# Second layer of a graph network: components of an outer product summed on TensorE in place of GpSimd

## The chip, the cores and the metric

The kernel runs on one core of a Trainium2 chip. The metric is the device time of one execution in microseconds (us). Three runs without a profile give a median of 7314.14 us. Everything is in fp32.

## The reference

Two graph layers run one after the other over the same 200,000 edges and 12,500 nodes of 160 features. A node's features are 64 scalars (s) and 32 vectors of 3 components (v). A layer makes a message for each edge, sums the messages by node, forms a bilinear update of each node, and normalises:

```
msg  = linear and bilinear functions of x[dst] and the edge's 4 attributes
agg  = segment_sum(msg, src)             # a0: 64 scalars, a1: 32 x 3
u0   = sum_uv xs[u] a0[v] Wu_ss[u,v,:] + sum_uv (sum_i xv[u,i] a1[v,i]) Wu_vv[u,v,:]
u1_i = sum_uv xs[u] a1[v,i] Wu_sv[u,v,:] + sum_uv xv[u,i] a0[v] Wu_vs[u,v,:]
x    = layernorm(x + x + u + linear(x))
```

The change is about the inner sum over i in the second term of u0. For each node it is a table q of 32 x 32 = 1024 numbers: the outer product of xv and a1 for each of the three components i, summed over the three. The table is then multiplied with Wu_vv (1024 x 64).

## The kernel before

The nodes are cut into 100 tiles of 125. There are three stages: the messages of the first layer, chunk by chunk; a sweep over node tiles of the first layer in which the messages of the second are made as well; and a sweep over the node tiles of the second layer alone (`node_sweep`, steps t = 0 to 101). Only the last is touched. It fills the span from about 6870 us to the end.

In step t of the last sweep the edges of tile t are summed, and tile n = t - 1 is updated. Each engine has a queue of its own, worked off in the order in which the code is written; they meet at semaphores. No planner reorders anything. The parts that matter:

- GpSimd, `node_step` (from line 651): for tile n, two mixed products `mixed_mul` (line 667, two instructions each) from ScalarE's copies `prods_sb`; then, for tile t, the outer product `outer` (line 647): q3 gets three blocks of 1024 per node, one for each component; then two additions (line 676) that sum blocks 1 and 2 into block 0. They count up the semaphore `q_part`.
- TensorE, `node_step` (from line 1157): six pairs of products `bilinear(0..5)` (lines 1177 and 1178), which alternate between two PSUM tiles `prods_ps`, so each waits until VectorE or ScalarE has used the one before the last. After the fifth comes `turn_q(0)`, then the sixth, then `sum_edges` (lines 1211 and 1212: 17 products of one-hot matrices with messages), `turn_q(1)`, `linear` (lines 1220 to 1224) and `turn_y` (lines 1231 to 1233).
- `turn_q(part)` turns half of q: 4 blocks of 128 columns by 125 nodes go to `turn_ps` as 128 x 125 each. In the second layer it is 4 transposes (line 1197) of the summed block. In the first layer it is 12 products with the identity (line 1200), three accumulated for each block, so that TensorE makes the sum over the components while it turns.
- ScalarE: copies the fifth and the sixth pair for GpSimd (`prods_out`, line 1467), copies turned q to SBUF (`turned_q`, line 1475), sums and turned y likewise (lines 1482 to 1502), then makes the one-hot matrices of the next tile (lines 1575 and 1581).
- VectorE: four rounds of product and sum for the scalar part (lines 954 and 960), its share of the mixed products (line 972), the sums of the mixed products (line 983, the second of which waits for GpSimd), and h (line 1000), which ends the tile.

Of the kernel before, what the change touches and what calls it, by code (L numbers as in the profile page):

```python
# [6 lines left out]
ALU = mybir.AluOpType  # L7
# [6 lines left out]
P = 128  # L14
# [3 lines left out]
HM = 125  # L18
# [36 lines left out]
VV = V * V  # L55
# [30 lines left out]
def build(nc, x, src, dst, attr, weights, out):  # L86
# [41 lines left out]
    with ExitStack() as whole:  # L128
        def sb(name, shape, dt=F32, ctx=whole):
            return ctx.enter_context(nc.sbuf_tensor(name, shape, dt))  # L130

        def sem(name):
            return whole.enter_context(nc.semaphore(name))

        def bank(name, n=1):
            return whole.enter_context(nc.psum_tensor(name, [P, 512 * n], F32))
# [3 lines left out]
        turn_ps = bank("turn_ps")  # L140
# [21 lines left out]
        for layer in range(2):  # L162
            t = Named()
# [77 lines left out]
        q3 = sb("q3", [P, 3 * VV])  # L241
# [30 lines left out]
        def layer_sems(layer):  # L272
            s = {}
            for n in ("hot", "edges_done", "y_out", "y_turned", "y_turned_out", "prods", "prods_used", "upd", "q_mul",
                      "q_turned", "q_turned_out", "lin", "lin_out", "h_ready", "deviation", "inverse", "normed",
                      "msg", "pay_out", "located", "slotted",
                      "t_turned", "t_turn_out", "t_mm", "t_out", "first_fill",
                      "sp_ids", "sp_link", "sp_index", "sp_rec", "sp_keys", "sp_tab", "sp_sum", "sp_old", "sp_put", "sp_done"):
                s[n] = sem(f"{n}_l{layer}")
            for n in (("picked", "pick_turned", "pick_out"), ("copied", "mixed_mul", "q_part"))[layer]:  # L280
                s[n] = sem(f"{n}_l{layer}")
            for n in ("msgs_in", "x_in", "stored", "spill_in", "rec_in", "t_stored", "filled"):
                s[n] = [sem(f"{n}{b}_l{layer}") for b in range(2)]
            for n in ("win_in", "scattered"):
                s[n] = [sem(f"{n}{q}_l{layer}") for q in range(4)]
            return s

        LS = [layer_sems(layer) for layer in range(2)]
        block = whole.enter_context(nc.Block())

# [35 lines left out]
        def within(k, lo, hi):  # L326

            return not isinstance(k, int) or lo <= k < hi
# [5 lines left out]
        def earlier(k):  # L334
            c, ck, cb = k
            return (c - 1, ck - 1, 1) if cb == 0 else (c - 1, ck, 0)
# [218 lines left out]
        def _(g):  # L555
# [23 lines left out]
            def scatter(layer, k, hh):  # L579

                c, ck, cb = k
                s, q = LS[layer], 2 * cb + hh
                g.wait_ge(s["located"], 2 * c + hh + 1)
                g.wait_ge(s["slotted"], 2 * c + hh + 1)
                if within(c, 2 - 2 * layer, STRIPS[layer]):
                    g.wait_ge(s["filled"][cb], 32 * ck + 32 * layer)
                for p in range(PAIRS):
                    g.wait_ge(s["pay_out"], 8 * c + 4 * hh + p + 1)
                    carry()
                    for j in (2 * p, 2 * p + 1):  # L590
                        g.indirect_dma_start(out=slots[layer][:, :], out_offset=bass.IndirectOffsetOnAxis(ap=slot[q][:, j:j + 1], axis=0),  # L591
                                             in_=pay[q][:, j, :], in_offset=None).then_inc(s["scattered"][q], 16)
# [44 lines left out]
            def outer(layer, k):  # L637

                n, nh, nb = k
                s = LS[layer]  # L640
                g.wait_ge(s["x_in"][nb], 16 * nh + 16)
                g.wait_ge(s["y_out"], 4 * n + 4)
                if within(n, 1, NT):
                    g.wait_ge(s["q_turned"], 2 * n)
                else:
                    g.wait_ge(s["sp_done"], 1)
                g.tensor_tensor(q3[0:HM, :].rearrange("p (i u v) -> p i u v", i=3, u=V),  # L647
                                xt[nb][0:HM, S:D].rearrange("p (u i) -> p i u", i=3).unsqueeze(3).broadcast_to([HM, 3, V, V]),
                                yv[nb][0:HM, :, 0:V].unsqueeze(2).broadcast_to([HM, 3, V, V]), ALU.mult).then_inc(s["q_mul"], 1)

            def node_step(layer, k, chunk):
                (t, half, b), (c, ck, cb) = k, chunk
                s = LS[layer]
                if layer == 0 and within(t, 1, NT + 1):
                    outer(0, (t - 1, half if b == 1 else half - 1, 1 - b))
                if layer == 1:
                    if within(t, 1, NT + 1):
                        n, nb = t - 1, 1 - b
                        for j in range(R1):
                            g.wait_ge(s["copied"], R1 * n + j + 1)  # L660
                            if j == 1:
                                g.wait_ge(s["upd"], RS_ALL * n + R0)
                            elif within(n, 1, NT):
                                g.wait_ge(s["upd"], RS_ALL * n - RS_ALL + R0 + 1)
                            wk = mixed_work[j][0:HM, :].rearrange("p (i w h k) -> p i h w k", i=3, h=2, k=V)
                            for i in range(DIRECT[1], 3):
                                mul = g.tensor_tensor(wk[:, i], prods_sb[j][0:HM, :].rearrange("p (h w k) -> p h w k", h=2, k=V),  # L667
                                                      yv[nb][0:HM, i, :].rearrange("p (h k) -> p h k", h=2).unsqueeze(2).broadcast_to([HM, 2, ROUND // KV, V]),
                                                      ALU.mult)
                            mul.then_inc(s["mixed_mul"], 1)  # L670
                    if within(t, 0, NT):
                        outer(1, k)
                        n = t
                        for j in range(2):
                            g.wait_ge(*((s["q_part"], 2 * n + 1) if j else (s["q_mul"], n + 1)))
                            add = g.tensor_tensor(q3[0:HM, 0:VV], q3[0:HM, 0:VV], q3[0:HM, VV * (j + 1):VV * (j + 2)], ALU.add)
                            add.then_inc(s["q_part"], 1)
                if layer == 0 and within(c, 0, NCH):
                    if isinstance(c, int) and c == 0:
                        g.wait_ge(LS[1]["first_fill"], 32 * PIECES)  # L680
                    if within(c, 1, NCH):
                        scatter(1, earlier(chunk), 1)
                    scatter(1, chunk, 0)

            spill(0)
            step_sweep(g, lambda k, chunk: node_step(0, k, chunk))
            scatter(1, (NCH - 1, NCH // 2 - 1, 1), 1)
            spill(1)
            node_sweep(g, lambda k, chunk: node_step(1, k, chunk))

        @block.vector
# [323 lines left out]
        def _(te):  # L1015
# [141 lines left out]
            def node_step(layer, k, chunk):  # L1157
                (t, half, b), (c, ck, cb) = k, chunk
                s, w = LS[layer], wt[layer]
                n, nb = t - 1, 1 - b  # L1160
                idn = ident[0:HM, 0:HM]
# [23 lines left out]
                def turn_q(part):  # L1185
                    if not nodes:
                        return
                    if part == 0:
                        te.wait_ge(*((s["q_mul"], n + 1) if layer == 0 else (s["q_part"], 2 * n + 2)))
                        if layer == 0 and within(t, 3, NT + 1):  # L1190
                            te.wait_ge(LS[1]["t_out"], t - 2)
                    else:
                        te.wait_ge(s["q_turned_out"], 2 * n + 1)
                    for j in range(QC // 2):
                        o = P * (j + part * QC // 2)
                        if layer == 1:
                            mm = te.transpose(turn_ps[:, HM * j:HM * j + HM], q3[0:HM, o:o + P], idn)
                            continue
                        for i in range(3):
                            mm = te.matmul(turn_ps[:, HM * j:HM * j + HM], q3[0:HM, VV * i + o:VV * i + o + P], idn, start=(i == 0), stop=(i == 2))  # L1200
                    mm.then_inc(s["q_turned"], 1)
# [41 lines left out]
                message(0, 3)  # L1243
                bilinear(4)
                turn_q(0)
                bilinear(5)
                sum_edges()
                turn_q(1)
                message(1, 0)
                linear()  # L1250
# [399 lines left out]
```

## Time and profile before

| | |
|---|---|
| median of 3 runs without a profile | 7314.14 us (7313.32 to 7323.62) |
| profiled execution, first to last instruction | 8954.3 us |
| mean granted clock of TensorE | 0.843 of full speed |
| second layer's node sweep, 7100 to 7300 us: PE, DVE, ACT, POOL busy | 155, 179, 130, 187 of 200 us |
| turns of q in the second layer (line 1197) | 4 transposes a half, 0.59 us |
| additions of q (line 676) | 2 a tile, 2.36 us each |

The profiled execution takes longer than one without a profile; of its time the page has the span alone, and that time is what durations below belong to. A matmul in fp32 shows as two records, a transpose as one. Names in a row are output<-inputs, then the shapes; in a timeline, what stands in brackets at the end is the idle time of that engine before the instruction, and what ended it. q is the program's q3, and turn_ps, node_ps and prods_ps are PSUM. picks_sb and work are the two buffers of mixed products. Instructions merged in a timeline row run from its start for its duration.

### The profile page before, as it was taken

What the parts mean: (1) busy time and instruction counts of PE and PEld (TensorE: products, weight loads), DVE (VectorE), ACT (ScalarE), POOL (GpSimd) and SP (SyncE); (2) the same over time, 40 slices, a digit from 0 to 9 for tenths busy, and PEclk for the clock granted to TensorE, in tenths of its full rate; (3) what the DMA queues carried; (4) which work ended last, traced back from release to release, by engine and by line L of the source; (5) the groups of instructions that cost most, each with busy time, mean ns of one, the idle gap of its engine ahead of it and who ended that gap; (6) DMA issues with size and microseconds to landing.
All of it is one profiled execution on the core that took longest, in us unless ns stands there. A gap on an engine that the chain in (4) does not pass through costs nothing.

```text
span 8954.3 us, 133249 instructions
## 1 busy us (share of the span) xinstructions
PE 6109.6 (68%) x33695; PEld 4449.2 (50%) x33695; DVE 5971.5 (67%) x7512; ACT 3773.2 (42%) x11870; POOL 5607.7 (63%) x3978
## 2 busy tenths in 40 slices
PE   3555555555554777777777777777775777777777
PEld 2444344444443555555555555555553555455544
DVE  4555555555555766666666666666663888888888
ACT  1222222222222444444444444444443666666665
POOL 1555555555556255555555555555556999999999
PEclk6777777777777889888888888888887999999999
DMA  6666666666664355555555555555543222222221
GB/s 185 188 192 196 190 193 191 190 192 189 194 193 135 114 175 181 174 180 168 174 176 175 173 179 176 171 173 176 169 149 102 84 83 77 84 84 82 78 84 63
DMA packets 692540, 1372.60 MB, mean 153 GB/s; under 512 B 106047, under 2 KB 500077, under 8 KB 666863
## 3 DMA queue, kind: packets, MB, share of 16 engines
q10 hardware_dynamic: 84636, 590.82, 21.2%
q1 hardware_dynamic: 455091, 499.42, 18.6%
q0 software_dynamic: 152736, 281.45, 9.5%
q8 instruction: 34, 0.56, 0.0%
q14 instruction: 43, 0.35, 0.0%
HBM read 587.20 MB, written 784.08 MB: 153 GB/s over the span
## 4 chain that ended last, share of the span: by engine, by line
PE 36%; issue 18%; another core or an unknown queue 16%; DVE 11%; ACT 8%; POOL 7%; ACTq 1%; SPq 1%; DMA 1%; DVEq 0%; POOLq 0%
PE turn_ps L1200 7%; PE node_ps L1211 7%; PE prods_ps L1177 6%; POOL work L667 4%; DVE upd L983 3%; PE m_ps L1110 3%; POOL picks_sb L667 3%; DVE work L954 2%; PE node_ps L1224 2%; DVE upd L960 2%; ACT onehot L1581 2%; PE s_ps L1110 2%; PE s_ps L1092 2%; PE node_ps L1110 2%
## 5 line engine op out<-in xcount | busy, mean ns | idle before, releaser
L591 POOL DMA_INDIRECT slots<-pay,slot x3136 | 3090.5, 986 | 2087.2 <-issue 1519.2
L647 POOL TENSOR_TENSOR q<-xt,yv 125x3072 f32<-125x3072 f32 x200 | 1094.1, 5470 | 1079.8 <-PE turn_ps L1200 1044.6
L954 DVE TENSOR_TENSOR work<-prods_ps,xt 125x1024 f32<-125x1024 f32 x800 | 958.5, 1219 | 1179.0 <-remote 538.6
L1178 PE MATMUL prods_ps<-w_bil,ys_t 64*125 64x512 f32 x2400 | 1419.6, 688 | 5.6 <-issue 5.6
L1211 PEld LDWEIGHTS node_ps<-msgs,onehot 128*125 128x125 f32 x6800 | 975.8, 195 | 326.3 <-issue 299.5
L1211 PE MATMUL node_ps<-msgs,onehot 128*125 128x160 f32 x6800 | 1022.0, 311 | 159.4 <-ACT onehot L1581 147.1
L983 DVE TENSOR_REDUCE upd<-work 125x48 f32<-125x3072 f32 x300 | 1005.9, 3353 | 127.2 <-POOL work L667 120.3
L1575 ACT ACTIVATE onehot<-node_iota,msgs 128x125 f32<-128x125 f32 x3400 | 1028.5, 393 | 103.6 <-POOLq L635 73.2
L1177 PE MATMUL prods_ps<-w_bil,a_t 64*125 64x512 f32 x1600 | 865.0, 643 | 248.9 <-DVE work L954 159.9
L960 DVE TENSOR_REDUCE upd<-work 125x16 f32<-125x1024 f32 x800 | 949.6, 1208 | 0.0
L1177 PE MATMUL prods_ps<-w_bil,ys_t 64*125 64x512 f32 x800 | 551.8, 776 | 517.2 <-issue 280.9
L1370 ACT COPY pay<-m_ps 128x320 f32<-128x320 f32 x784 | 335.0, 427 | 1224.1 <-remote 930.5
L972 DVE TENSOR_TENSOR work<-prods_ps,yv 125x1024 f32<-125x1024 f32 x700 | 818.7, 1217 | 38.3 <-remote 15.8
L1110 PE MATMUL m_ps<-win,picks_sb 125*128 125x160 f32 x3136 | 684.0, 347 | 219.0 <-ACT pay L1370 127.3
L1092 PE MATMUL s_ps<-ident,picks_sb 128*125 128x128 f32 x1568 | 342.5, 356 | 652.5 <-ACT picks_sb L1348 548.7
L1200 PEld LDWEIGHTS turn_ps<-ident,q 125*128 125x128 f32 x4800 | 676.3, 227 | 158.9 <-issue 151.9
L1110 PEld LDWEIGHTS m_ps<-win,picks_sb 125*128 125x128 f32 x3136 | 530.0, 219 | 381.0 <-issue 247.7
L1200 PE MATMUL turn_ps<-ident,q 125*128 125x125 f32 x4800 | 702.7, 312 | 16.1 <-issue 11.2
L833 DVE TENSOR_TENSOR before<-before,prods_ps 128x100 f32<-128x100 f32 x392 | 100.1, 255 | 895.7 <-remote 634.5
L1092 PEld LDWEIGHTS s_ps<-ident,picks_sb 128*125 128x125 f32 x1568 | 290.2, 254 | 688.2 <-issue 376.2
L1110 PE MATMUL node_ps<-win,picks_sb 125*128 125x160 f32 x1568 | 394.9, 388 | 327.8 <-issue 208.5
L1177 PEld LDWEIGHTS prods_ps<-w_bil,a_t 64*125 64x125 f32 x1600 | 252.5, 185 | 594.0 <-DVE work L954 337.1
(231 smaller groups left out, 11233.4 us busy)
## 6 DMA issues: line engine op xcount, KB each, us to landing
msgs<-slots ACTq DMA_DIRECT2D x200, 1428.0 KB, 6.1
slots<-zero ACTq DMA_DIRECT2D x183, 1386.0 KB
win<-table SPq DMA_DIRECT2D x784, 160.0 KB
picks<-picks_sb SPq DMA_DIRECT2D x196, 512.0 KB
picks_sb<-picks SPq DMA_DIRECT2D x196, 512.0 KB
table<-tab SPq DMA_DIRECT2D x200, 350.0 KB
slots<-pay,slot POOLq DMA_INDIRECT x3136
spill_in<-spill_sums SPq DMA_DIRECT2D x200, 80.0 KB, 2.0
```

The lines of the kernel that those rows point to most:

```text
L591: g.indirect_dma_start(out=slots[layer][:, :], out_offset=bass.IndirectOffsetOnAxis(ap=slot[q][:, j:j + 1], axis=0), in_=pay[q][:, j, :], ...
L647: g.tensor_tensor(q3[0:HM, :].rearrange("p (i u v) -> p i u v", i=3, u=V), xt[nb][0:HM, S:D].rearrange("p (u i) -> p i u", i=3).unsqueeze( ...
L954: ve.tensor_tensor(third(r), prods_ps[r % 2][0:HM, :].rearrange("p (w u) -> p w u", u=S), X[:, 0:S].unsqueeze(1).broadcast_to([HM, ROUND / ...
L960: ve.tensor_reduce(upd[0:HM, ROUND // S * (r - 1):ROUND // S * r], third(r - 1), AX_X, ALU.add).then_inc(s["upd"], 1)
L972: ve.tensor_tensor(wk[:, i, :, :].rearrange("p w (h k) -> p h w k", h=2), prods_ps[r % 2][0:HM, :].rearrange("p (h w k) -> p h w k", h=2, ...
L983: ve.tensor_reduce(upd1[:, :, w0:w0 + ROUND // KV], mixed_part(r), AX_X, ALU.add).then_inc(s["upd"], 1)
L1110: mm = te.matmul(to[:, D * j:D * j + D], (pick_b[q] if layer else pick_n[hh])[0:WROWS, P * (2 * p + j):P * (2 * p + j) + P], win[q][0:WROW ...
L1177: te.matmul(prods_ps[r % 2][0:HM, 0:512], upper, w.bil[0:S, 512 * r:512 * r + 512], start=True, stop=True)
L1178: te.matmul(prods_ps[r % 2][0:HM, 512:1024], ys_t[S:P, :], w.bil[S:P, 512 * r:512 * r + 512], start=True, stop=True).then_inc(s["prods"], 1)
L1200: mm = te.matmul(turn_ps[:, HM * j:HM * j + HM], q3[0:HM, VV * i + o:VV * i + o + P], idn, start=(i == 0), stop=(i == 2))
L1211: te.matmul(node_ps[0:HM, 0:D], onehot[:, j, :], msgs[b][:, j, 0:D], start=(j == 0), stop=False)
L1575: last = ac.activation(onehot[:, j, :], node_iota[:, :], ACT.Square, bias=msgs[b][:, j, LOCAL:LOCAL + 1], scale=-1.0)
```

## The change

The two additions leave GpSimd's step, and the semaphore `q_part` goes. In the second layer `turn_q` then does what it did in the first: it waits for the outer product (`q_mul`) and forms each turned block by three accumulating products with the identity.

```diff
-            for n in (("picked", "pick_turned", "pick_out"), ("copied", "mixed_mul", "q_part"))[layer]:
+            for n in (("picked", "pick_turned", "pick_out"), ("copied", "mixed_mul"))[layer]:
...
                     if within(t, 0, NT):
                         outer(1, k)
-                        n = t
-                        for j in range(2):
-                            g.wait_ge(*((s["q_part"], 2 * n + 1) if j else (s["q_mul"], n + 1)))
-                            add = g.tensor_tensor(q3[0:HM, 0:VV], q3[0:HM, 0:VV], q3[0:HM, VV * (j + 1):VV * (j + 2)], ALU.add)
-                            add.then_inc(s["q_part"], 1)
...
                     if part == 0:
-                        te.wait_ge(*((s["q_mul"], n + 1) if layer == 0 else (s["q_part"], 2 * n + 2)))
+                        te.wait_ge(s["q_mul"], n + 1)
...
                     for j in range(QC // 2):
                         o = P * (j + part * QC // 2)
-                        if layer == 1:
-                            mm = te.transpose(turn_ps[:, HM * j:HM * j + HM], q3[0:HM, o:o + P], idn)
-                            continue
                         for i in range(3):
                             mm = te.matmul(turn_ps[:, HM * j:HM * j + HM], q3[0:HM, VV * i + o:VV * i + o + P], idn, start=(i == 0), stop=(i == 2))
                     mm.then_inc(s["q_turned"], 1)
```

## Rows read from the trace of the kernel before

**Rows 1.** Two stretches of the second layer. Columns: stretch, length, busy us (instructions) of PE, PEld, DVE, ACT, POOL, granted clock, DMA share, GB/s.

```profile
7100.00:7300.00 200.00, 155.11 (x898) 102.03 (x894) 179.32 (x136) 129.90 (x351) 186.68 (x69) 0.97 0.23 77
8500.00:8700.00 200.00, 155.52 (x911) 104.12 (x912) 178.12 (x134) 128.72 (x357) 187.39 (x68) 0.97 0.25 85
```

**Rows 2.** Timeline of one tile: start, duration, engine, line, tiles, count, idle before.

```profile
8513.99 2.36 DVE L954 TENSOR_TENSOR work<-prods_ps,xt 125x1024 f32<-125x1024 f32 x2 [0.29 <-PE prods_ps L1178]
8515.33 4.80 POOL L676 TENSOR_TENSOR q<-q 125x1024 f32<-125x1024 f32 x2
8518.66 0.69 PE L1177 MATMUL prods_ps<-w_bil,ys_t 64*125 64x512 f32 x1 [1.13 <-DVE work L954]
...
8519.91 1.01 ACT L1467 COPY pay<-prods_ps 125x1024 f32<-125x1024 f32 x1 [1.38 <-PE prods_ps L1178]
8520.18 0.65 PE L1197 MATMUL turn_ps<-ident,q 125*128 125x125 f32 x4 [0.39 <-POOL q L676]
8520.92 0.69 PE L1177 MATMUL prods_ps<-w_bil,ys_t 64*125 64x512 f32 x1
8521.09 4.69 POOL L667 TENSOR_TENSOR picks_sb<-pay,yv 125x1024 f32<-125x1024 f32 x2 [0.96 <-ACT pay L1467]
8521.98 4.88 PE L1211 MATMUL node_ps<-msgs,onehot 128*125 128x160 f32 x34
8525.75 4.66 POOL L667 TENSOR_TENSOR work<-pay,yv 125x1024 f32<-125x1024 f32 x2
8526.97 0.59 PE L1197 MATMUL turn_ps<-ident,q 125*128 125x125 f32 x4
8528.48 0.53 PE L1220 MATMUL node_ps<-xt,ident 125*125 125x160 f32 x2 [0.92 <-ACT q_t L1475]
...
8530.51 3.35 DVE L983 TENSOR_REDUCE upd<-work 125x48 f32<-125x3072 f32 x1 [1.21 <-POOL work L667]
8532.36 0.69 PE L1177 MATMUL prods_ps<-w_bil,a_t 64*125 64x512 f32 x1 [0.89 <-ACT v_t L1502]
8534.71 2.36 DVE L954 TENSOR_TENSOR work<-prods_ps,xt 125x1024 f32<-125x1024 f32 x2 [0.42 <-PE prods_ps L1178]
```

**Rows 3.** Chain that ended last, four tiles, shares by line.

```profile
by line: issue 25.4%; POOL work L667 20.7%; DVE upd L983 16.8%; POOL picks_sb L667 11.9%; DVE upd L960 7.2%; DVE work L954 6.2%; PE prods_ps L1177 5.6%; ACT pay L1467 5.1%; DVE h L1000 1.0%; DVEq L320 0.3%; DVEq L944 0.2%; POOLq L641 0.2%; 
```

**Rows 4.** Groups of instructions on POOL, 7000 to 8900 us: count, busy, mean, idle.

```profile
L676 POOL TENSOR_TENSOR q<-q 125x1024 f32<-125x1024 f32 x183 | 432.2, 2362 | 14.3
L667 POOL TENSOR_TENSOR picks_sb<-pay,yv 125x1024 f32<-125x1024 f32 x184 | 431.4, 2366 | 109.1 <-ACT pay L1467 109.1
```

**Rows 5.** Timeline of PE in the first layer, the turns by products of line 1200.

```profile
6126.09 4.20 PE L1200 MATMUL turn_ps<-ident,q 125*128 125x125 f32 x24
...
6136.93 2.84 PE L1200 MATMUL turn_ps<-ident,q 125*128 125x125 f32 x24
6139.60 0.71 PE L1110 MATMUL m_ps<-win,picks_sb 125*128 125x160 f32 x4
```

**Rows 6.** Timeline of PE in the first layer, a product pair of L1177/L1178 and what follows.

```profile
6111.28 0.69 PE L1177 MATMUL prods_ps<-w_bil,a_t 64*125 64x512 f32 x1
...
6112.33 0.81 PE L1110 MATMUL m_ps<-win,picks_sb 125*128 125x160 f32 x4
```

**Rows 7.** Timeline, first tile of the second layer, where VectorE waits for PE.

```profile
6866.45 0.69 PE L1177 MATMUL prods_ps<-w_bil,a_t 64*125 64x512 f32 x1 [0.67 <-ACT v_t L1502]
...
6867.73 2.36 DVE L954 TENSOR_TENSOR work<-prods_ps,xt 125x1024 f32<-125x1024 f32 x2 [21.57 <-PE prods_ps L1178]
```

**Rows 8.** Timeline of VectorE, first product of the second and of the last tile.

```profile
6890.15 2.36 DVE L954 TENSOR_TENSOR work<-prods_ps,xt 125x1024 f32<-125x1024 f32 x2 [1.32 <-PE prods_ps L1178]
...
8929.36 2.35 DVE L954 TENSOR_TENSOR work<-prods_ps,xt 125x1024 f32<-125x1024 f32 x2 [0.19 <-DVE h L1000]
```

**Rows 9.** Stretches of PE: length, busy (count), granted clock, DMA share, GB/s.

```profile
7163.00:7164.00 1.00, 1.00 (x4) 0.50 0.00 0
7160.00:7180.00 20.00, 16.25 (x93) 0.91 0.25 85
```

## The prediction

> **What bounds the kernel now.** The change is in the second layer, which holds a hundred tiles of nodes, so I read the stretches first. There GpSimd (POOL) is busy 187 of 200 us, VectorE (DVE) 178 and TensorE (PE) 155 [rows 1]. By these shares GpSimd is the bound, and an edit that takes additions from it looks like a gain. The other views say otherwise. In the chain of waits through that layer [rows 3] GpSimd stands with the products of line 667 alone; the additions (line 676) and the outer product (line 647) are not in it. The idle time before each group says why: GpSimd sat idle 109.1 us before 92 of the first products of line 667, waiting for ScalarE's copy, 1.19 us a tile [rows 4]. An engine that waits once in every tile is not the bound of that tile.
>
> The timeline of one tile [rows 2] gives the loop that is. VectorE starts its products at 8513.99. TensorE gets the bank back and starts the fifth pair (the fifth `bilinear`) at 8518.66, ScalarE copies at 8519.91, GpSimd multiplies from 8521.09 and again from 8525.75 to 8530.41, VectorE sums from 8530.51 for 3.35, adds up h and starts the next tile at 8534.71. That is 20.72 us, and from the second tile to the last the mean is (8929.36 - 6890.15) / 98 = 20.81 us [rows 8]. The additions run at 8515.33 to 8520.13 beside this loop, and end 0.96 us before GpSimd can go on.
>
> The second loop is TensorE's own, and it is nearly as long. TensorE takes its work in written order. From the start of the first pair to VectorE's first product is 1.28 us where VectorE waits for it [rows 7]; from there to the sixth pair 6.93; to the sum over edges 1.06; to the second half of the turns 4.99; to the linear part 1.51 (the turns 0.59, then ScalarE's copy of q_t); to the next tile's first pair 3.88 [rows 2]. Sum 19.65 us. So TensorE has 20.72 - 19.65 = 1.07 us of room in a tile. This is the number that decides.
>
> **The change part by part.** *Removed:* two additions a tile on GpSimd, 2 x 2.36 = 4.7 us [rows 4]. They lie beside the loop that binds, so this is worth nothing by itself: GpSimd waits 4.7 us longer for the same copy. The two semaphore waits that go with them cost GpSimd no time that the chain shows. TensorE's wait for the sum goes too (0.39 us of idle before the turns, [rows 2]): it now waits for the outer product, which ends at 8509.77 + 5.47, well before the fifth pair at 8518.66, so that wait is never late.
>
> *Added:* each half of the turns is 12 accumulating products in place of 4 transposes. The second layer has no such row, but the first layer runs exactly this code: 24 records, two to a product in fp32, take 2.84 us at full clock, and the next instruction starts 2.67 us after the first of them [rows 5]. Four transposes take 0.59 [rows 2]. The bounds: below, half the records (if one pass were enough, as for a transpose) 1.4 us; above, the 4.20 us of the turns that met the lower clock [rows 5]. I take 2.84, the nearest row: same instruction, same shapes.
>
> *What moves.* First half: a pair of products and what follows are 1.05 apart at full clock [rows 6]. So the turns start 1.05 after the fifth pair and the sixth pair starts 2.67 after that: 4.67 + 1.05 + 2.67 = 8.39 us after VectorE's first product, where it is 6.93 today. Costs 1.46, since part of the turns fills a gap in which TensorE waited for VectorE. Second half: it stands behind the edge sum with ScalarE's copy and the linear part waiting for it, nothing covers it, and it costs 2.84 - 0.59 = 2.25 us. Queued behind both on TensorE are the sum over edges, the linear part, the turns of y and the next tile's first pair, for which VectorE waits.
>
> TensorE's loop becomes 1.28 + 8.39 + 1.06 + 4.99 + (1.51 + 2.25) + 3.88 = 23.36 us. The other loop stays at 20.7: the sixth pair, 1.46 us later, gives its copy at about 8524.6, and GpSimd wants it at 8525.75, so it just fits. GpSimd's outer product has to wait for the second half of the turns, which frees q3: they end 8.39 + 1.06 + 4.99 + 2.84 = 17.3 us into the tile, and GpSimd has multiplied until 8530.41, 16.4 us into it. That is 0.9 us of waiting, with some 7.6 us of room behind the outer product. So TensorE becomes the bound, GpSimd falls to about 15 of 23.4 us, and a tile costs 23.36 - 20.81 = 2.55 us more. Times 98 intervals: 250 us. The first interval adds 2 us (its sixth pair was late already, for the sum); the last tile has no edges to sum and stays as it is. Together 252 us. On the profiled execution's span of 8954.3 us that makes 9206. The runs without a profile have a median of 7314.1, 1640 us less, and no row says in which stage this difference lies; the second layer moves little by DMA (share 0.25, [rows 1]), so I carry the 252 us over unchanged: 7566 us.
>
> *The clock.* Today the granted clock falls to 0.50 (1.2 in place of 2.4 GHz) for a part of some tiles, after the gap that TensorE has while VectorE works; 9 of 30 stretches of 20 us have 0.91 to 0.93 on average, like the one at 7160 [rows 9]. In the new loop that gap is shorter, because VectorE then waits for TensorE and not the other way round. The sum above has no slow tile in it. If three in ten stay slow over the first half of the turns, that adds 98 x 0.3 x (4.20 - 2.84) = 40 us. The Trainium skill speaks of this: "TensorE: Matmul & The Clock Gate", Part 4, says that transposes do not count as activity for the clock as matmuls do. By that rule the new turns would keep the clock up where the transposes did not, and the sum would stay free of slow tiles; if the rule is wrong here, the 40 us come on top. No row of before tells the two apart, since transposes and products alternate in every tile.
>
> **The rivals.**
> 1. *TensorE has the room, no change.* If a product of fp32 data with the identity ran in one pass, a half would be 1.42 us: the sixth pair at 4.67 + 1.05 + 1.33 = 7.05, the second half 0.83 longer, the loop 19.65 + 0.12 + 0.83 = 20.6, hidden behind the 20.7. Time 7314. For it: the transposes do so. Against: 24 records to 12 products in the first layer [rows 5].
> 2. *Faster: GpSimd is the bound in the runs without a profile.* Place: the first product of line 667. If the copy is there before GpSimd is free, each us taken off GpSimd counts until TensorE's loop of 19.65 us binds: 98 x (20.72 - 19.65) = 105 us, 7209. It decides only where GpSimd's 1.19 us of idle per tile is an effect of the profile and TensorE's additions stay within 1.07 us. For it: the busy share. Against: the idle rows [rows 4] and 3.7 us of added work on TensorE.
> 3. *Slower than forecast: TensorE at the lower clock in every tile.* The first half of the turns follows the stretch where the clock drops. 98 x 1.36 = 133 us more, 7699. For it: [rows 9]. Against: more work and shorter gaps.
> 4. *Part of the added time is taken up*: a copy or a queue that the sum counts in full overlaps by half of the 2.55 us. 125 us, 7439. Against: both loops are read from starts, which hold such overlaps already.
>
> **How the numbers follow.** Forecast 0.70, no change 0.05, faster 0.03, lower clock 0.12, partly hidden 0.10. The predicted time is that of the first, 7566. Its own range, with 0 to 40 us for the clock and 0.25 us a tile either way for the pieces of the sum, is 7540 to 7630. To leave out no more than 2 in 10 I go some way toward both neighbours: 7485 to 7665. What a measurement of this kernel can tell from no change is about 0.2%, 15 us. Slower takes the forecast, the lower clock and the partly hidden case: 0.92; same 0.05; faster 0.03.
>
> **What the profile of the changed kernel would show.** Right: the time between VectorE's first products near 23.4 us; turns in the second layer with 24 records and 2.84 us in each half; GpSimd near 63% busy in that layer, its idle 0.9 us before line 647 and near 7.6 us before line 667; the chain of waits passing through the turns, the edge sum and the linear part; VectorE waiting for the first pair in each tile and no longer for GpSimd. The first layer as before. The forecast is wrong if the turns take under 1.6 us a half, if VectorE's wait after the second GpSimd product (1.21 us, [rows 2]) is still what precedes each h, or if the interval stays at 20.8 us.

## The result, and the profile after

The changed kernel takes 7553.97 us (median of 4 runs, 7547.9 to 7564.73) against 7314.73 us: ratio 1.0329, 95% interval 1.0314 to 1.0343. The forecast was 7566 us; 239 us were added where 252 were expected. Right in sign and in cause; in size too, though by some luck, since two errors of 0.2 us a tile in the sum cancelled. What follows is mostly about two things that the forecast had only in part, how the 1.07 us of room is shared and what the clock does.

The page of the changed kernel: the span, and the busy time of each engine with its share and its instructions.

```profile
span 7546.2 us, 140957 instructions
...
PE 6083.8 (81%) x37695; PEld 4602.3 (61%) x37695; DVE 5929.2 (79%) x7512; ACT 3750.8 (50%) x11870; POOL 5141.0 (68%) x3778
```

The profiled execution of before has a span of 8954.3 us, 1640 us over its timed runs, and this one's is 7546.2, like its own timed runs (7547.9). The excess isn't the profile's doing, since in another session the kernel before took 8944 us without one (last run below). So only the second layer's sweep is compared between the two. The excess lay in the stages before that sweep: its first h starts at 6888.5 us there and at 5236.7 here, 1652 us apart. GpSimd's row of line 591 has 968 us of it: 1119.4 us of idle time before the scattering DMAs, where the page of before has 2087.2, while each of them took 986 ns in both.

```profile
L591 POOL DMA_INDIRECT slots<-pay,slot x3136 | 3092.2, 986 | 1119.4 <-issue 1020.8
```

The stretch of the second layer's sweep (columns as in [rows 1]): TensorE is busy 86% of it, GpSimd 63%, and the granted clock is 1.00 where it was 0.97.

```profile
5400.00:7000.00 1600.00, 1378.96 (x9129) 1031.78 (x9130) 1277.54 (x963) 931.69 (x2549) 1014.56 (x345) 1.00 0.21 73
```

One tile, in the rows that answer to [rows 2] (start, duration, engine, line, tiles, count, idle before). Line 949 is what was 954, 1172 was 1177, 1192 is the turns, 1203 the edge sum, 978 the sums of the mixed products, 995 h, 1459 the copies of the pairs, 1467 the copy of turned q (1475 before), 1494 the last copy of turned y, 1212 the start of the linear part and 1216 its end.

```profile
7006.40 0.33 DVE L995 TENSOR_TENSOR h<-node_ps,upd 125x160 f32<-125x160 f32 x1 [1.21 <-PE node_ps L1216]
7007.45 0.69 PE L1172 MATMUL prods_ps<-w_bil,a_t 64*125 64x512 f32 x1 [0.91 <-ACT v_t L1494]
7008.62 2.36 DVE L949 TENSOR_TENSOR work<-prods_ps,xt 125x1024 f32<-125x1024 f32 x2 [1.89 <-PE prods_ps L1173]
...
7013.29 0.69 PE L1172 MATMUL prods_ps<-w_bil,ys_t 64*125 64x512 f32 x1 [1.13 <-DVE work L949]
7014.35 2.94 PE L1192 MATMUL turn_ps<-ident,q 125*128 125x125 f32 x24
7015.72 4.67 POOL L667 TENSOR_TENSOR picks_sb<-pay,yv 125x1024 f32<-125x1024 f32 x2 [7.37 <-ACT pay L1459]
...
7017.22 0.69 PE L1172 MATMUL prods_ps<-w_bil,ys_t 64*125 64x512 f32 x1
7018.27 4.88 PE L1203 MATMUL node_ps<-msgs,onehot 128*125 128x160 f32 x34
...
7023.27 2.84 PE L1192 MATMUL turn_ps<-ident,q 125*128 125x125 f32 x24
7025.12 3.35 DVE L978 TENSOR_REDUCE upd<-work 125x48 f32<-125x3072 f32 x1 [1.13 <-POOL work L667]
7026.14 0.57 ACT L1467 COPY q_t<-turn_ps 128x500 f32<-128x500 f32 x1 [2.32 <-PE turn_ps L1192]
7026.19 5.47 POOL L647 TENSOR_TENSOR q<-xt,yv 125x3072 f32<-125x3072 f32 x1 [1.17 <-PE turn_ps L1192]
7026.85 0.53 PE L1212 MATMUL node_ps<-xt,ident 125*125 125x160 f32 x2 [0.74 <-ACT q_t L1467]
...
7030.68 0.69 PE L1172 MATMUL prods_ps<-w_bil,a_t 64*125 64x512 f32 x1 [0.84 <-ACT v_t L1494]
7031.85 2.36 DVE L949 TENSOR_TENSOR work<-prods_ps,xt 125x1024 f32<-125x1024 f32 x2 [1.82 <-PE prods_ps L1173]
```

VectorE's first product starts at 7008.62 and the next tile's at 7031.85: 23.23 us (20.72 in [rows 2]). VectorE waited 1.82 us for the first pair. The 0.42 us of [rows 2] stand under the same name, but that pair had begun 2.35 us earlier (8532.36 to 8534.71), and 1.28 are enough [rows 7], so it was not what VectorE waited for there. The turns have 24 records, 2.94 and 2.84 us. Ahead of h VectorE has 1.21 us of idle time, ended by the linear part (row at 7006.40). Its wait for GpSimd ahead of the second sum is still there (1.13 us, row at 7025.12; 1.21 in [rows 2]), but it no longer decides: in [rows 2] the sum, h and the next tile's start followed on it with at most 0.42 us of idle time between them, and here both of the waits for TensorE come after it. The chain of waits over three and a half tiles, shares by line, answers to [rows 3]:

```profile
by line: PE turn_ps L1192 24.2%; PE node_ps L1203 18.1%; issue 16.6%; PE prods_ps L1172 13.6%; PE node_ps L1216 8.7%; DVE work L949 5.7%; ACT q_t L1467 2.9%; PE node_ps L1212 2.7%; PE node_ps L1204 1.2%; ACT v_t L1494 1.1%; PE node_ps L1213
```

The turns, the edge sum, the pairs and the linear part hold at least 68% of it, and no GpSimd instruction is in the chain. GpSimd's rows over the sweep (columns as in [rows 4]): its idle time before the copy's product is 715.8 us over 98 tiles, 7.3 a tile, where [rows 4] had 1.19.

```profile
L647 POOL TENSOR_TENSOR q<-xt,yv 125x3072 f32<-125x3072 f32 x99 | 541.4, 5469 | 130.5 <-PE turn_ps L1192 114.5 <-ACT yv L1475 16.0
L667 POOL TENSOR_TENSOR picks_sb<-pay,yv 125x1024 f32<-125x1024 f32 x196 | 458.7, 2359 | 715.8 <-ACT pay L1459 715.8
```

Who waited for whom, in total over the sweep (engine, line, whom it waited for: us, times, longest):

```profile
DVE work L949 <- PE prods_ps L1173: 205.3, 101, 20.2
DVE h L995 <- PE node_ps L1216: 118.8, 98, 1.2
```

### The profile page after: what moved, and what is told of

It is laid out like the page before. It is cut to its first block, busy times and chain, and to the rows that moved or that the text cites. A ratio compares the mean times of both kernels' runs of the same rounds, so it can differ in the third digit from the quotient of the medians.

```text
span 7546.2 us, 140957 instructions
## 1 busy us (share of the span) xinstructions
PE 6083.8 (81%) x37695; PEld 4602.3 (61%) x37695; DVE 5929.2 (79%) x7512; ACT 3750.8 (50%) x11870; POOL 5141.0 (68%) x3778
## 4 chain that ended last, share of the span: by engine, by line
PE 59%; DMA 11%; issue 10%; ACT 7%; DVE 5%; POOL 4%; ACTq 2%; SPq 1%; POOLq 0%; DVEq 0%
PE turn_ps L1192 15%; PE node_ps L1203 13%; PE prods_ps L1172 11%; DMA slots<-pay,slot 9%; PE node_ps L1216 5%; PE m_ps L1105 4%; POOL slots L591 3%; PE s_ps L1105 2%; DVE work L949 2%; ACT onehot L1573 2%; PE node_ps L1105 2%; ACT q_t L1467 2%; PE node_ps L1212 1%; PE turn_ps L1056 1%; ACTq L350 1%
## 5 line engine op out<-in xcount | busy, mean ns | idle before, releaser
L591 POOL DMA_INDIRECT slots<-pay,slot x3136 | 3092.2, 986 | 1119.4 <-issue 1020.8
L1173 PE MATMUL prods_ps<-w_bil,ys_t 64*125 64x512 f32 x2400 | 1296.3, 634 | 0.0
L1192 PEld LDWEIGHTS turn_ps<-ident,q 125*128 125x128 f32 x9600 | 1107.0, 192 | 153.7 <-issue 152.2
L1192 PE MATMUL turn_ps<-ident,q 125*128 125x125 f32 x9600 | 1156.1, 277 | 0.0
L1203 PEld LDWEIGHTS node_ps<-msgs,onehot 128*125 128x125 f32 x6800 | 931.9, 188 | 238.4 <-issue 224.5
L1203 PE MATMUL node_ps<-msgs,onehot 128*125 128x160 f32 x6800 | 978.0, 302 | 82.6 <-ACT onehot L1573 82.6
L667 POOL TENSOR_TENSOR picks_sb<-pay,yv 125x1024 f32<-125x1024 f32 x200 | 468.0, 2360 | 729.6 <-ACT pay L1459 729.6
L1467 ACT COPY q_t<-turn_ps 128x500 f32<-128x500 f32 x400 | 230.1, 575 | 635.5 <-PE turn_ps L1192 635.5
L1172 PE MATMUL prods_ps<-w_bil,ys_t 64*125 64x512 f32 x800 | 448.1, 640 | 119.8 <-DVE work L949 119.8
L1340 ACT COPY picks_sb<-s_ps 125x512 f32<-125x512 f32 x392 | 229.4, 585 | 532.3 <-PE s_ps L1087 296.4
L1573 ACT ACTIVATE onehot<-onehot,ones_f 128x500 f32<-128x500 f32 (+3 forms) x400 | 471.8, 1179 | 3.4
L667 POOL TENSOR_TENSOR work<-pay,yv 125x1024 f32<-125x1024 f32 x200 | 467.7, 2360 | 0.0
```

The source lines that it names most:

```text
L1172: te.matmul(prods_ps[r % 2][0:HM, 0:512], upper, w.bil[0:S, 512 * r:512 * r + 512], start=True, stop=True)
L1173: te.matmul(prods_ps[r % 2][0:HM, 512:1024], ys_t[S:P, :], w.bil[S:P, 512 * r:512 * r + 512], start=True, stop=True).then_inc(s["prods"], 1)
L1203: te.matmul(node_ps[0:HM, 0:D], onehot[:, j, :], msgs[b][:, j, 0:D], start=(j == 0), stop=False)
```

## The experiments

Each was timed beside the kernel before on the same chip, and the ratios are to that. The diffs are shortened. A tile's mean time is that from the first to the last h of the sweep in the profile, over 99 intervals: 20.81 us before, 23.28 in the changed kernel.

**Each half of the edit alone.** First the removal without the products:

```diff
-        add = g.tensor_tensor(q3[..block 0..], q3[..block 0..], q3[..block j + 1..], ALU.add)   # both additions
-        te.wait_ge(s["q_part"], 2 * n + 2)
+        te.wait_ge(s["q_mul"], n + 1)
         mm = te.transpose(turn_ps[...], q3[0:HM, o:o + P], idn)        # block 0 alone
```

> Only the removal: GpSimd makes no additions, and TensorE turns the first component alone by transposes (the sum over components is left out). Theory (two loops: one from VectorE over ScalarE and GpSimd of 20.7 us a tile, one of TensorE of 19.65): the additions lay beside the first loop, so 7315 us, within 15 us of the kernel before; GpSimd's idle time before line 667 grows from 1.2 to about 6 us a tile. Rival (GpSimd was the bound in runs without a profile): the tile falls to TensorE's 19.65 us, 7210 us.

Measured 7313.89 us, ratio 0.9996 (0.9987 to 1.0006): nothing. A tile took 20.78 us. GpSimd's rows of this kernel show where the 4.7 us went, into waiting for the copy: 551.5 us before 91 of the first products, 6.1 a tile.

```profile
L667 POOL TENSOR_TENSOR picks_sb<-pay,yv 125x1024 f32<-125x1024 f32 x182 | 426.9, 2366 | 551.5 <-ACT pay L1462 551.5
```

Then the products without the removal:

```diff
-        mm = te.transpose(turn_ps[...], q3[0:HM, o:o + P], idn)
+        for i in range(3):
+            mm = te.matmul(turn_ps[...], q3[0:HM, VV * i + o:VV * i + o + P], idn, start=(i == 0), stop=(i == 2))
```

> Only the products: the additions on GpSimd stay, and the turns are 12 products a half all the same (the second and third component are then counted twice). Theory: TensorE's loop is 23.3 us as in the changed kernel, GpSimd's 19.7 us of work fits under it, 7554 us within 15. Rival (GpSimd's work takes part in the time, and taking it off gave part of the cost back): slower than the changed kernel by more than 15 us, up to the 4.7 us a tile of the additions, 8015 us.

Measured 7559.25 us, ratio 1.0331 (1.0314 to 1.0348), a tile of 23.25 us: the whole cost of the change (ratio 1.0329), with the additions still there. GpSimd's rows of it: the additions take their 2.36 us each and GpSimd still waits 202.9 us over 82 tiles for the copy.

```profile
L676 POOL TENSOR_TENSOR q<-q 125x1024 f32<-125x1024 f32 x164 | 387.6, 2363 | 12.9
L667 POOL TENSOR_TENSOR picks_sb<-pay,yv 125x1024 f32<-125x1024 f32 x164 | 384.2, 2365 | 202.9 <-ACT pay L1464 202.9
```

The two together show it: the removal is worth nothing, the products are the 239 us. That GpSimd was the bound in runs without a profile is ruled out.

**Half of q each way.** GpSimd sums 512 columns in place of 1024, TensorE transposes these and makes products of the others.

```diff
-   q3[0:HM, 0:VV], q3[0:HM, 0:VV], q3[0:HM, VV * (j + 1):VV * (j + 2)]
+   q3[0:HM, lo:hi], q3[0:HM, lo:hi], q3[0:HM, VV * (j + 1) + lo:VV * (j + 1) + hi]   # a half
-   if layer == 1:                       # transpose
+   if layer == 1 and part == which:     # transpose; the other part by products
```

> The first half of q by products, the second half summed on GpSimd (two additions of 512 columns) and transposed. Theory: the first half of the turns fills a gap of TensorE and costs 1.46 us of TensorE's loop, 19.65 + 1.46 = 21.1 us a tile against 20.8, 98 x 0.3 = 29 us: 7345 us (7315 to 7360). Rival (each half costs the same, half of the 239 us measured): 7434 us.

> The reverse: the first half summed on GpSimd and transposed, the second half by products. Theory: the second half stands uncovered between the edge sum and ScalarE's copy, 19.65 + 2.25 = 21.9 us a tile, 98 x 1.1 = 107 us: 7421 us (7400 to 7440). Together with the other half more than either sum, since 1.07 us of room is spent once only: 1.46 + 2.25 - 1.07. Rival (half of the cost each): 7434 us here and in the other.

Measured 7362.57 us (1.0065, 1.0048 to 1.0082) with the first half by products, 7400.69 us (1.0117, 1.0100 to 1.0134) with the second. That each half costs half, 7434, is ruled out for both; 46 and 84 us sum to 130, not to 239, since each of the two spends the same room: 98 x 1.07 = 105 us of it, counted once more, make 235. The sizes were off: I expected 29 (7362.57 lies outside the range that I gave, by 3 us) and 107 (7400.69 lies at the end of its range). TensorE's rows of the first of the two kernels, then of the second, say why:

```profile
6212.79 2.94 PE L1202 MATMUL turn_ps<-ident,q 125*128 125x125 f32 x24
6215.66 0.69 PE L1177 MATMUL prods_ps<-w_bil,ys_t 64*125 64x512 f32 x1
...
6221.71 0.59 PE L1199 MATMUL turn_ps<-ident,q 125*128 125x125 f32 x4
6223.22 0.53 PE L1222 MATMUL node_ps<-xt,ident 125*125 125x160 f32 x2 [0.92 <-ACT q_t L1477]
```

```profile
6202.46 0.65 PE L1197 MATMUL turn_ps<-ident,q 125*128 125x125 f32 x4
6203.66 0.69 PE L1177 MATMUL prods_ps<-w_bil,ys_t 64*125 64x512 f32 x1 [0.55 <-DVE work L954]
...
6209.72 2.84 PE L1200 MATMUL turn_ps<-ident,q 125*128 125x125 f32 x24
6213.29 0.53 PE L1220 MATMUL node_ps<-xt,ident 125*125 125x160 f32 x2 [0.74 <-ACT q_t L1475]
```

By products, the first half keeps the sixth pair away for 2.87 us (6212.79 to 6215.66), not for the 2.67 of [rows 5]. Nearly all tiles took 21.1 to 21.4 us, and seven, in which pairs ran at the lower clock, 22.6 to 23.2. These seven make the mean 21.31 and are some 13 of the 46 us. The second half adds 2.25 us, but the wait for ScalarE's copy behind it shrinks from 0.92 to 0.74 us, so linear starts only 3.57 us after the turns (1.51 before): 2.06, not 2.25; a tile took 21.6 us.

**Fewer records.**

```diff
-  two additions;  for i in range(3)
+  g.tensor_tensor(q3[0:HM, 0:VV], q3[0:HM, 0:VV], q3[0:HM, VV:2 * VV], ALU.add).then_inc(s["q_part"], 1)
+  for i in (0, 2)                      # two accumulating products for each block
```

> One addition on GpSimd (components 0 and 1), and two accumulating products for each block on TensorE (16 records a half). Theory: TensorE's loop scales with the records: first half 4.67 + 1.06 + 2.0 = 7.7 us to the sixth pair in place of 6.9, second half 1.9 us in place of 0.6, 21.4 to 21.5 us a tile against 20.8: 98 x 0.65 = 64 us, 7380 us (7360 to 7400). Rival (a fixed cost of the switch from transposes to products, whatever their number): as the changed kernel, 7554 us.

Measured 7380.43 us, ratio 1.0096 (1.0079 to 1.0113), 21.48 us a tile. The two halves of this kernel:

```profile
6202.01 2.05 PE L1195 MATMUL turn_ps<-ident,q 125*128 125x125 f32 x16
...
6210.04 1.94 PE L1195 MATMUL turn_ps<-ident,q 125*128 125x125 f32 x16
```

16 records take 1.94 us where 24 take 2.84, 0.11 for each further one: the cost goes by records. A fixed cost of the switch to products would have left the time at that of the changed kernel, and is ruled out.

**Time off TensorE's loop.** If TensorE binds, its wait for turned q (0.74 us of idle) should be time.

```diff
 def linear():
-    te.wait_ge(s["q_turned_out"], 2 * n + 2)
     te.matmul(... xt ...)     te.matmul(... v_t ...)     te.matmul(... ys_t ...)
+    te.wait_ge(s["q_turned_out"], 2 * n + 2)      # second layer
     for j in range(QC): te.matmul(... q_t ...)
```

> The changed kernel, but in the linear part TensorE waits for ScalarE's copy of turned q only after the three products that don't read it. Theory (TensorE's loop binds): TensorE's idle of 0.74 us a tile behind the second half of the turns goes, 98 x 0.7 = 70 us off, 7485 us (7470 to 7500). Rival (another engine's chain binds, and TensorE's waits are only its idle time): 7554 us.

Measured 7603.57 us, ratio 1.0397 (1.0379 to 1.0414): 50 us slower than the changed kernel, against both theories. The profile of this kernel has the gap gone and something new. TensorE's rows, and below them stretches of it (length, busy, granted clock, DMA share, GB/s):

```profile
6210.08 2.84 PE L1192 MATMUL turn_ps<-ident,q 125*128 125x125 f32 x24
6212.75 0.44 PE L1213 MATMUL node_ps<-xt,ident 125*125 125x160 f32 x2
...
6216.78 1.13 PE L1172 MATMUL prods_ps<-w_bil,a_t 64*125 64x512 f32 x1 [0.92 <-ACT v_t L1497]
6217.71 1.05 PE L1172 MATMUL prods_ps<-w_bil,a_t 64*125 64x512 f32 x1
...
6240.66 1.21 PE L1172 MATMUL prods_ps<-w_bil,a_t 64*125 64x512 f32 x1 [0.91 <-ACT v_t L1497]
```

```profile
6241.00:6244.00 3.00, 3.00 (x8) 0.50 0.21 53
5400.00:7000.00 1600.00, 1433.51 (x8905) 0.93 0.21 71
```

Linear now starts 2.67 us after the turns. But the clock is at 0.50 over the next tile's first pairs, 1.2 in place of 2.4 GHz, in 88 of 99 tiles, and such a tile takes 23.89 us, most of them the same to 0.02. The changed kernel has a clock of 1.00 over the same stretch of time. The other 11 tiles of this kernel took 22.1 to 22.8 us. To tell the clock from the wait itself, I filled gaps of TensorE with products that nobody reads:

```diff
+def filler(count):
+    for _ in range(count):
+        te.matmul(m_ps[:, 0:HM], ident[0:HM, :], idn, start=True, stop=True)
 bilinear(3)
+filler(3)
 bilinear(4)            # the fifth pair
 ...
 turn_y()
+filler(3)
```

> The kernel with the late wait (7604 us, granted clock halved at the same place of nearly every tile, 23.89 us a tile), with products added that nobody reads in two gaps of TensorE: three before the fifth pair, three behind the turns of y. Theory (the late wait did shorten TensorE's loop to 22.5 us, and the lower clock took that and more): the gaps filled, the clock stays up, 22.5 us a tile, 7480 us (7465 to 7510). Rival (the loss has another cause, as the late wait itself): 7600 us or more.

Measured 7480.06 us, ratio 1.0224 (1.0207 to 1.0241), 22.48 us a tile. Its stretch:

```profile
5400.00:7000.00 1600.00, 1532.71 (x10329) 1174.82 (x10327) 1321.85 (x995) 961.23 (x2629) 1053.90 (x357) 1.00 0.22 76
```

So the late wait is worth 74 us as TensorE's loop says, and the clock took 124 us (7603.57 - 7480.06). What was shown is that the clock does it and that more work in two gaps cures it; which of the gaps decides wasn't separated. Nor is it shown why the late wait brought the clock down: in a tile of this kernel TensorE's idle stretches over 0.35 us are 0.92, 0.42 and 1.13 us long, and the changed kernel, at 1.00, has 0.91, 0.47 and 1.13 and the 0.74 besides.

**The loop over GpSimd, shortened.** The two loops point to a faster kernel than either: leave the additions on GpSimd, and bring its first mixed product forward, so that GpSimd goes on right after them.

```diff
+ORDER = ((0, 1, 2, 3, 4, 5), (0, 1, 4, 2, 3, 5))     # pairs by layer; banks by place in this order
 # VectorE, second layer, after the first sum:
+    mixed_mul(R0)
 # ScalarE, second layer: squares at the end of a step, then in the next one
     prods_out(0)
+    selections(1, t + 1, 0, BLOCKS).then_inc(LS[1]["hot"], 1)
     turned_q(0)
```

> The kernel before (additions on GpSimd, transposes), with the first mixed pair moved ahead: TensorE makes the pairs in the order 0, 1, 4, 2, 3, 5, VectorE uses them in that order, ScalarE copies pair 4 between the squares and the selection of the one-hot matrices. Theory (the loop over VectorE, ScalarE and GpSimd binds before): GpSimd starts right after its additions, its 19.6 us of work are the bound, 19.8 us a tile against 20.8, 7217 us (7200 to 7250). In this kernel the additions are in the time. Rival (TensorE's loop or VectorE's queue is as long as the other): no gain, 7300 us or more.

> The kernel of the run before this one with the late wait for turned q too. Theory: TensorE's loop (about 19.1 us) lies under GpSimd's 19.8, so the late wait is worth nothing here: within 15 us of the run before. Rival (TensorE binds there): 50 to 70 us faster than it.

Measured 7325.05 us (1.0016, 1.0007 to 1.0026) and, with the late wait, 7260.98 us (0.9929, 0.9912 to 0.9945). Neither came out as expected: the reorder alone gained nothing, and the late wait, expected to be worth nothing there, was worth 64 us. The tiles of the second kernel fall in two groups, about half at 19.6 us, close to the 19.8 that I expected of the reorder, the others at 20.5 to 21.7; the reorder made a gap of 2.4 us on TensorE before the pair at the fifth place, and in the slow tiles the clock is down behind it:

```profile
6205.69 1.23 DVE L960 TENSOR_TENSOR picks_sb<-prods_ps,yv 125x1024 f32<-125x1024 f32 x1 [1.08 <-ACT pay L1488]
6207.05 1.21 PE L1195 MATMUL prods_ps<-w_bil,a_t 64*125 64x512 f32 x1 [2.38 <-DVE picks_sb L960]
```

The pair's passes take 1.21 us there (0.69 at full clock). TensorE's loop, lengthened in this way, binds in those tiles, so time off it counts after all. The clock isn't all of it: with the reorder alone, 35 of 99 tiles took 20.0 to 20.2 us and only three less, where 54 took 19.6 to 20.0 with the late wait. Filling that gap, then also the one behind the turns of y:

```diff
+filler(7)
 bilinear(4)          # the pair at the fifth place
 ...
 turn_y()
+filler(3)            # in the second of the two runs only
```

> The reordered kernel with the late wait (7261 us; 19.61 us in tiles at full clock, 20.8 to 21.7 in the others), with seven products that nobody reads in the gap of 2.4 us before the pair at the fifth place. Theory (only the clock keeps it from 19.6): 19.65 us in every tile, 7314 - 98 x 1.15 = 7200 us (7185 to 7225). Rival (the added 1.6 us are work in TensorE's loop like any other): 7261 us or more.

> As the run before, with three more such products in the gap of 0.9 us behind the turns of y. Theory: the same 7200 us if the first gap alone decides the clock, and nothing lost, since 0.67 us fit in the gap. Rival (the last products end after ScalarE's copy and delay the next tile's first pair): 10 to 30 us more than the run before.

Measured 7200.18 us, ratio 0.9837 (0.9821 to 0.9854), and 7203.56 us (0.9847, 0.9830 to 0.9863), the same within their intervals. Nearly every tile took 19.6 us (95 of 99 under 19.8 in the first of the two). TensorE's rows: 14 records that nobody reads, 1.83 us, and the pair behind them at full clock.

```profile
6201.51 1.83 PE L1259 MATMUL m_ps<-ident 125*128 125x125 f32 x14
...
6203.27 0.69 PE L1195 MATMUL prods_ps<-w_bil,a_t 64*125 64x512 f32 x1
```

This is the fastest kernel here, 1.6% under the one before and 4.7% under the changed one. GpSimd's rows in it have 17 us of idle time in 1800, and over the stretch GpSimd is busy 1587 of 1600 us and VectorE 1515:

```profile
L677 POOL TENSOR_TENSOR picks_sb<-pay,yv 125x1024 f32<-125x1024 f32 x184 | 431.8, 2370 | 0.0
L677 POOL TENSOR_TENSOR work<-pay,yv 125x1024 f32<-125x1024 f32 x184 | 431.7, 2371 | 2.8 <-DVE upd L995 2.8
L686 POOL TENSOR_TENSOR q<-q 125x1024 f32<-125x1024 f32 x182 | 431.6, 2372 | 14.3
```

```profile
5400.00:7000.00 1600.00, 1412.64 (x8740) 989.25 (x8739) 1514.82 (x1142) 1096.78 (x3014) 1587.30 (x572) 1.00 0.25 87
```

In the chain of waits over four tiles of it no other engine than GpSimd appears:

```profile
by line: issue 27.7%; POOL q L657 27.4%; POOL work L677 17.1%; POOL picks_sb L677 15.3%; POOL q L686 12.3%; POOLq L685 0.3%; POOLq L330 0.2%; POOLq L651 0.2%; POOLq L652 0.2%; POOLq L674 0.2%; POOLq L670 0.1%
```

GpSimd looks like the bound at last. The last run took its additions away there:

```diff
 # of the 7200 us kernel
-    two additions on GpSimd
-    te.wait_ge(s["q_part"], 2 * n + 2)
+    te.wait_ge(s["q_mul"], n + 1)       # and transposes of block 0 alone
```

> The 7200 us kernel without GpSimd's additions, TensorE turning the first component alone by transposes (the sum over components is left out, as in the first of these runs). There GpSimd works 19.6 of 19.61 us a tile and waits for nothing. Theory: now, and only now, the additions are in the time; without them the tile falls to what VectorE's queue takes, 18.6 us of work and some 0.7 us of waits, 19.3 us: 98 x 0.3 = 30 us less than 7200, 7170 us (7150 to 7190). Rival (the additions never count): 7200 us.

In this run the stages ahead of the second layer took longer for every kernel, the one before too, which stood at 8943.68 us; this one stood at 8820.27 us, ratio 0.9877 (0.9839 to 0.9915), 123 us under it, with an interval of some 34 us either way, where the 7200 us kernel was 116 under its own. The tile doesn't depend on those stages (20.81 us in the profile of before, which had them slow, and 20.78 in that of the removal alone, which had not); it took 19.73 us against 19.66. My 30 us were not there. 77 of the 99 tiles took 19.4 to 19.8 us, 19.55 on average, 0.08 under the 19.63 of such tiles with the additions; the other 22 took 20.0 to 20.6, the clock at 0.91 in some stretches of them (7400 to 7420, 7440 to 7460), and took back more than the others gained. Stretch and waits of this kernel:

```profile
6900.00:8500.00 1600.00, 1418.94 (x8680) 991.17 (x8680) 1506.42 (x1135) 1092.13 (x2998) 1201.50 (x406) 0.99 0.26 87
```

```profile
POOL picks_sb L677 <- ACT pay L1489: 218.2, 81, 3.3
POOL work L677 <- DVE upd L990: 180.3, 81, 3.2
```

GpSimd falls to 75% and waits 398 us over 81 tiles, for ScalarE's copy and for VectorE's sums, and VectorE is busy 94%, nearly the 95% of before. GpSimd's 99% were as little the bound by themselves as the 187 of 200 us in [rows 1]: the loop through VectorE's queue was nearly as long. From 7500 to 7820 us, where no tile is slow, VectorE is busy 303.7 of 320 us and waits for others 11.9, 0.7 us a tile as I took it; the 0.27 us a tile between its instructions are what the sum of 19.3 had left out.

## Why the prediction was right

- *The bound before.* Right: the removal alone gave 0.9996. The idle time before line 667 (1.19 us a tile) was the evidence, and it grew to 6.1 us when the work went. This holds of the additions only: GpSimd's products of line 667 are part of the loop that bound [rows 3].
- *The turns' price.* 24 records, 2.84 us taken from the first layer; measured 2.84 in the second half and 2.94 in the first. What the first half keeps from the sixth pair was read as 2.67 and is 2.87.
- *TensorE's loop.* Forecast 23.36 us, measured 23.23. By pieces, forecast and measured (7007.45 to 7030.68): first pair to VectorE 1.28, 1.17; to the fifth pair 4.67, 4.67; to the turns 1.05, 1.06; to the sixth pair 2.67, 2.87; to the edge sum 1.06, 1.05; to the second half 4.99, 5.00; to linear 3.76, 3.58; to the next first pair 3.88, 3.83. The errors of 0.2 in the first half and in the copy's wait cancel, which is luck: the first half keeps the sixth pair away for longer than the first layer's row had it, and the wait for the copy behind the second half shrinks. What is left of the difference, 0.13 us a tile, makes up about the 13 us between forecast and result.
- *What is left of the room.* Measured for the halves alone 46 and 84 us, for both at once 239. The room of about one us was spent once, as forecast; my sizes of 29 and 107 had the same two errors, which there don't cancel, and the first has the seven tiles at the lower clock besides.
- *GpSimd.* Forecast 0.9 and 7.6 us of idle time, 63% busy; measured 1.17, 7.37 and 63%.
- *The clock.* The sum had no slow tile in it, and the changed kernel has two (24.7 us), where 9 of 30 stretches before were low [rows 9]. The reason I gave was a shorter gap while VectorE works. The gap did shrink, from 1.65 us ahead of the third pair in the kernel before (first row) to 0.46 in the changed one:

```profile
8535.99 0.69 PE L1177 MATMUL prods_ps<-w_bil,a_t 64*125 64x512 f32 x1 [1.65 <-DVE work L954]
7033.13 0.69 PE L1172 MATMUL prods_ps<-w_bil,a_t 64*125 64x512 f32 x1 [0.46 <-DVE work L949]
```

But its length alone can't be the reason: the gaps of the kernel with the late wait are no longer than the changed kernel's (0.92, 0.42 and 1.13 us), and it lost the clock in nearly every tile. The rule of the Trainium skill ("TensorE: Matmul & The Clock Gate", Part 4), that transposes do not count as activity as matmuls do, fits the changed kernel as well, but is not shown by it: the kernel with the late wait has the same products and a clock of 0.93, and the 7200 us kernel turns q by transposes and has 1.00, with its gap filled. In both it was filling gaps with products that brought the clock back, whatever turned q; what made it fall stays open. What the lower clock costs where nearly every tile meets it, priced at 133 us in the third rival, was 124 in the kernel with the late wait; that was at another place of the tile, so it doesn't confirm the price.

## What to carry to other kernels

An engine at 94% busy that waits once a tile for somebody else does not bind by its share, and work taken off it ahead of that wait only makes the wait longer; before taking work off it, add up the loops through each engine's queue, and look at how much room the engine that is to get the work has in its own (here 1.07 us, for 3.7 us of added time). Work in a gap is cheap only until the gap is full. And when an edit moves TensorE's gaps, look at the granted clock in the tiles before the edit is judged: 74 us gained were read as 50 lost, and useless products in the right gap made a kernel 61 us faster.

## What the runs showed of the hardware

- An fp32 product with the identity, 125 to 128 partitions by 125 columns, takes two records, accumulating or not, and each further record adds 0.11 us (second halves 16 in 1.94 us and 24 in 2.84; first halves 16 in 2.05 and 24 in 2.94; 14 that don't accumulate in 1.83); a transpose takes one, four in 0.59 us.
- The clock can settle into step with a loop: 23.89 us a tile in 88 of 99 tiles, with 0.50 at the same place of each. TensorE's longest idle stretch in such a tile was 1.13 us. That it does so was not expected; why it holds there stays open. Six products that nobody reads, in two gaps, brought it to 1.00.
- The same kernel takes 7314 or 8944 us in different sessions. The difference is in the stages ahead of the second layer's sweep, those with the scattering DMAs; the tiles of that sweep took 20.81 us in the slow kind, and 20.78 in the quick kind with the additions removed, which the timed runs show to be worth nothing. What makes a session slow stays open.
